# Routing and experts of a graph layer in one block instead of two, with one sequence of 98 seat transfers

## Chip, cores and metric

One core of one Trainium2 chip runs the whole program as one launch. The metric is the device time in microseconds (us). Engine names are those of the profile: PE is TensorE, DVE is VectorE, ACT is ScalarE, POOL is GpSimd, SP is SyncE, which here only issues DMAs. A "q" behind a name (SPq, POOLq) means the queue of that engine.

## What is computed

```python
xn = layernorm(x)                                  # x: 6250 x 256, fp32
x = x + gnn(xn, edges) + mix(xn)                   # two graph convolutions of three passes each; linear attention
f = layernorm(x)
rh = relu(f @ router_w1 + router_b1)               # 256 -> 128
p = softmax(rh @ router_w2 + router_b2)            # 6 experts
top_w, top_i = top_k(p, 2); w = softmax(top_w)
e_out = (relu(relu(f @ w1[e] + b1[e]) @ w2[e] + b2[e])) @ w3[e] + b3[e]   # 256 -> 256 -> 256 -> 256
x = x + sum over the two chosen experts e of w[e] * e_out[e]
```

The change touches only the last part, from the decoder of the graph network to the end (the mixture of six experts, of which each of the 6250 tokens uses two).

## The kernel before, in words

Some 2,890 us of the program are the graph part (function `sums`). The change leaves it alone, save that the 128 x 12,544-word tile `split`, which the passes used, gets a second use afterwards.

**Routing** is the function `final`, one block (L2211) in which the five engines each have an instruction list and meet through semaphores. The 49 token tiles of 128 rows go through it in 7 batches (`BATCHES`) of 7 tiles (`SUB`). For each batch PE decodes and projects, DVE adds and takes the row statistics, ACT normalises, PE turns the tiles and computes the six router logits (L2320), DVE picks the two experts (class `Choice`), and PE counts, with small products against triangular and full matrices, how many earlier tokens took the same expert (`ranked`, L2327 to L2332). From these counts DVE computes for each token two seats, that is, two row numbers in a DRAM table `row_d` that is sorted by expert, and writes them as integers (L2526, semaphore `l_idx`). POOL then sends each tile's rows (256 values, the scale and shift of the normalisation, two weights, the first expert, the token's number) to their seats: two indirect transfers per tile (L2263, `scattered`), 14 per batch. In the block of before POOL does this for the first six batches alone, 84 transfers.

After the last batch DVE does the **planning** (L2570 to L2596): from the number of tokens of each expert it makes, for each of 38 slots of 384 rows, the first row and the expert (`table`), the expert again as a number per partition (`expert_of`) and an offset that throws rows past an expert's end out of range (`beyond`). Then the block ends: every engine drains, reports to a common semaphore, and goes on when all have.

**Experts** is the function `experts`, a second block (L2650). Its POOL list begins with the 14 transfers that were left, those of the last batch (`late`, L2743). Its SP list issues the weights of slots 0 and 1 (`pack_in`, L2668, 898 KB each), waits until all 98 transfers have landed (`l_sent`), and issues the rows of slots 0 to 2 (`rows_in`, L2663). Each of these needs a row number or expert number that SP loads from `table` (L2654). For each slot DVE normalises the rows (L2692, L2694), PE turns them (L2801), ACT copies them back, PE does three layers (L2810, L2818, L2826) with ACT's relu between, DVE adds the last bias and weighs (L2716, L2720), and POOL adds the three tiles into `out` with indirect transfers (L2751). Three slots are in flight (`BUF` = 3). SP, DVE, ACT and PE run most of the 38 slots in loops of three slots; POOL's list is written out. At the end SP waits for the last of POOL's transfers, and the block ends as the first did.

Of the kernel before, what the change touches and what calls it, by code (L numbers as in the profile page):

```python
# [7 lines left out]
ALU = mybir.AluOpType  # L8
# [9 lines left out]
P = 128  # L18
# [154 lines left out]
def gps_layer(nc, a, out):  # L173
# [19 lines left out]
    with ExitStack() as whole:  # L193
# [17 lines left out]
        final(nc, a, out, sem, ident, mix, words(other)[:, NP:2 * NP], words(other), ahead, xnT_d, params, row_d, pack_d)  # L211
# [1915 lines left out]
def final(nc, a, out, sem, ident, mix, hidden, spare, ahead, xnT_d, params, row_d, pack_d):  # L2127
# [11 lines left out]
    with ExitStack() as main:  # L2139
# [5 lines left out]
        l_sent = sem("g_scattered")  # L2145
        LATE = range((BATCHES - 1) * SUB, TILES)

        with ExitStack() as ph:
# [44 lines left out]
            d_ps = [bank(f"d_ps{h}", [P, WIN]) for h in range(HB)]  # L2193
            rec_ps = [bank(f"rec_ps{n}", [P, D]) for n in range(2)]
            tn_ps = [bank(f"tn_ps{n}", [P, D]) for n in range(2)]
            lg_ps = bank("lg_ps", [P, SUB * EXP])
            rank_ps = bank("rank_ps", [P, MANY + 1, EXP])
# [13 lines left out]
            with nc.Block() as block:  # L2211
                @block.sync
                def _(sp):
# [29 lines left out]
                    sp.wait_ge(l_kept, 16 * (BATCHES + 1))  # L2243

                @block.gpsimd
                def _(pool):
# [18 lines left out]
                    for n in range(BATCHES - 1):  # L2265
                        scattered(n)

                @block.tensor
                def _(pe):
# [81 lines left out]
                    ranked(BATCHES - 1)  # L2351

                @block.scalar
                def _(act):
# [63 lines left out]
                    ratio(BATCHES - 1)  # L2418

# [178 lines left out]

        experts(nc, out, sem, ident, spare, table, beyond, expert_of, rows, seat_of, LATE, l_sent, row_d, pack_d)


def experts(nc, out, sem, ident, spare, table, beyond, expert_of, tokens, seat_of, late, l_sent, row_d, pack_d):
# [7 lines left out]
    with ExitStack() as ph:  # L2610
        def sb(name, shape, dt=F32):
            return ph.enter_context(nc.sbuf_tensor(name, shape, dt))

        def bank(name, shape):
            return ph.enter_context(nc.psum_tensor(name, shape, F32))

        rows = sb("slot_rows", [P, BUF, ST, RW])
        meta = sb("slot_meta", [P, BUF, ST, 4])
        share = sb("slot_share", [P, BUF, 3, ST])
        done = sb("slot_out", [P, BUF, ST, D])  # L2620
        space = Carve(spare)
        pack = space.take(BUF, PACK)
        idx = sb("slot_idx", [P, BUF, ST], mybir.dt.uint32)
        xlT = space.take(BUF, 2, SLOT)
        h1 = space.take(2, SLOT)
        h2 = space.take(2, SLOT)
        t_ps = [bank(f"t_ps{n}", [P, 2, 2, P]) for n in range(2)]
        one_ps = [bank(f"one_ps{n}", [P, SLOT]) for n in range(2)]
        two_ps = [bank(f"two_ps{n}", [P, SLOT]) for n in range(2)]
        out_ps = [bank(f"out_ps{n}", [P, D]) for n in range(2)]  # L2630
        k_rows, k_pack, k_sent = ([sem(f"{n}{b}") for b in range(BUF)] for n in ("k_rows_in", "k_weights_in", "k_scattered"))
        k_xl, k_turn, k_turnc, k_one, k_onec, k_two, k_twoc, k_out, k_bias, k_done, k_meta, k_share, k_idx = (
            sem(n) for n in ("k_normed", "k_turned", "k_turned_copied", "k_first", "k_first_copied", "k_second", "k_second_copied", "k_third",
                             "k_third_biased", "k_out_ready", "k_meta", "k_share", "k_idx"))

        def weight(b, n):
            return pack[:, b, n * 2 * D:(n + 1) * 2 * D].rearrange("p (c h) -> p c h", c=2)

        def bias_of(b, n, hc):
            at = 6 * D + 2 * n + hc  # L2640
            return pack[:, b, at:at + 1]

        def bias3(b):
            return pack[:, b, 6 * D + 4:6 * D + 4 + D]

        def sent(s):

            return 16 * ST * (s // BUF + 1)

        with nc.Block() as block:  # L2650
            @block.sync
            def _(sp):
                def entry(s, col):
                    _, got = nc.values_load_multi_w_load_instructions(  # L2654
                        table[0:1, bass.ds(s, 1), col:col + 1].rearrange("o s c -> o (s c)"), engines=[mybir.EngineType.SP], min_val=0,
                        max_val=(row_d.shape[0] - SLOT, EXPERTS - 1)[col],
                        skip_runtime_bounds_check_because="rows of a region and a number of an expert")
                    return got[0]

                def rows_in(s, b):  # L2660
                    at = entry(s, 0)
                    sp.wait_ge(k_turn, s + 1)
                    sp.dma_start(rows[:, b, :, :], row_d[bass.ds(at, SLOT), :].rearrange("(t p) c -> p t c", p=P)).then_inc(k_rows[b], 16)  # L2663

                def pack_in(s, b):
                    e = entry(s, 1)
                    sp.wait_ge(k_done, s * ST + ST)
                    sp.dma_start(pack[:, b, :], pack_d[bass.ds(e, 1), :, :].rearrange("o p c -> (o p) c")).then_inc(k_pack[b], 16)  # L2668

                sp.sem_inc(k_turn, BUF)  # L2670
                sp.sem_inc(k_done, BUF * ST)
                for s in range(2):
                    pack_in(s, s)
                sp.wait_ge(l_sent, 16 * 2 * TILES)
                for s in range(BUF):
                    rows_in(s, s)
                with sp.Fori(0, LOOPED) as q:
                    for b in range(BUF):
                        rows_in(q * BUF + (b + BUF), b)
                        pack_in(q * BUF + (b + 2), (b + 2) % BUF)  # L2680
                for s in range(LOOPED * BUF, STEPS - 2):
                    if s + BUF < STEPS:
                        rows_in(s + BUF, s % BUF)
                    pack_in(s + 2, (s + 2) % BUF)
                for s in range(STEPS - BUF, STEPS):
                    sp.wait_ge(k_sent[s % BUF], sent(s))

            @block.vector
            def _(dve):
                def normed(q, b):  # L2690
                    dve.wait_ge(k_rows[b], q * 16 + 16)
                    nc.vector.tensor_copy(meta[:, b, :, :], rows[:, b, :, D + 2:D + 6]).then_inc(k_meta, 1)  # L2692
                    for t in range(ST):
                        m = nc.vector.tensor_scalar(rows[:, b, t, 0:D], rows[:, b, t, 0:D], rows[:, b, t, D:D + 1], rows[:, b, t, D + 1:D + 2], ALU.mult, ALU.add)  # L2694
                    m.then_inc(k_xl, 1)

                def prepared(q, b):

                    s = q * BUF + b
                    if not (isinstance(q, int) and q == 0):  # L2700
                        dve.wait_ge(k_sent[b], q * (16 * ST))
                    dve.wait_ge(k_meta, s + 1)
                    e = expert_of[:, bass.ds(s, 1)]
                    first, second, both = (share[:, b, n, :] for n in range(3))
                    nc.vector.scalar_tensor_tensor(first, meta[:, b, :, FIRST], e, meta[:, b, :, W1], ALU.is_equal, ALU.mult).then_inc(k_share, 1)
                    nc.vector.scalar_tensor_tensor(second, meta[:, b, :, FIRST], e, meta[:, b, :, W2], ALU.not_equal, ALU.mult).then_inc(k_share, 1)
                    nc.vector.tensor_tensor(idx[:, b, :], meta[:, b, :, ID], beyond[:, bass.ds(s, 1), :].rearrange("p o t -> p (o t)"), ALU.add).then_inc(k_idx, 1)
                    dve.wait_ge(k_share, s * 3 + 2)
                    nc.vector.tensor_tensor(both, first, second, ALU.add).then_inc(k_share, 1)
                    dve.wait_ge(k_idx, s + 1)  # L2710

                def finished(q, b):
                    s = q * BUF + b
                    for t in range(ST):
                        dve.wait_ge(k_out, s * ST + (ST + t + 1))
                        nc.vector.tensor_tensor(done[:, b, t, :], out_ps[t % 2][:, :], bias3(b), ALU.add).then_inc(k_bias, 1)  # L2716
                    dve.wait_ge(k_share, s * 3 + 3)
                    for t in range(ST):
                        dve.wait_ge(k_bias, s * ST + (ST + t + 1))
                        nc.vector.tensor_scalar(done[:, b, t, :], done[:, b, t, :], share[:, b, 2, t:t + 1], None, ALU.mult).then_inc(k_done, 1)  # L2720

                for b in range(BUF):
                    normed(0, b)
# [9 lines left out]
                for s in range(LOOPED * BUF, STEPS):  # L2733
                    prepared(s // BUF, s % BUF)
                    if s + BUF < STEPS:
                        normed((s + BUF) // BUF, s % BUF)
# [137 lines left out]
```

## Time and profile before

| what | us |
|---|---|
| median of 3 runs (3478.55 to 3478.9) | 3478.65 |
| the profiled execution | 3479.78 |
| its span, first to last instruction | 3477.8 |
| PE busy in it | 3163.9 (91%) |
| POOL busy in it | 923.7 (27%) |

The profiled execution took 1.98 us more than its span, and 1.13 us more than the median. Times below are positions in the span. The columns of a row of the timeline are: start, duration, engine, line, operation, output <- inputs, shapes, count, and in brackets the idle time of the engine before it and what ended it. Several instructions of a kind that follow each other are merged into one row with their count.

### The profile page before, as it was taken

The page shows a single profiled execution, that of the slowest core. Times are in us where ns is not written, and L with a number is a line of the kernel's source. Part 1 is how long each engine was busy: PE and PEld are TensorE (multiplying, and loading weights), DVE is VectorE, ACT ScalarE, POOL GpSimd, SP SyncE. Part 2 cuts the span into 40 slices and gives each one's busy share as a digit, 9 for nine tenths or more (in the row PEclk, how much of TensorE's full clock was granted, in tenths as well). Part 3 has the DMA queues.
Part 4 walks back from the last instruction along what each step waited for, and adds up shares of the span by engine and source line. Part 5 has one row for each costly group of instructions (what it writes and reads, how often), then busy time and mean ns, then how long its engine had stood idle before and what let it go on. Part 6 is the DMA issues. An engine that isn't in the chain of part 4 may idle for free. (4 is left out here: it accounts for less than half of the span.)

```text
span 3477.8 us, 48392 instructions
## 1 busy us (share of the span) xinstructions
PE 3163.9 (91%) x16879; PEld 1851.0 (53%) x16880; DVE 1374.4 (40%) x5337; ACT 787.6 (23%) x1656; POOL 923.7 (27%) x912
## 2 busy tenths in 40 slices
PE   7798999999998898898999999999999999728998
PEld 3464666566554444454455555555555556516775
DVE  7846777777732222221222221222221005433443
ACT  3444555555520000000000000000000003313332
POOL 2000000000006666636666630000000000454555
PEclk9897999999998999999999999999999999869999
DMA  7212465556457666756666668888889995336886
GB/s 185 72 65 85 149 235 208 179 198 234 179 234 246 196 222 203 235 179 203 211 211 223 212 188 291 291 290 292 291 292 319 303 302 160 118 111 168 204 203 138
DMA packets 252700, 723.78 MB, mean 208 GB/s; under 512 B 36437, under 2 KB 159817, under 8 KB 250472
## 3 DMA queue, kind: packets, MB, share of 16 engines
q1 hardware_dynamic: 184298, 595.84, 51.1%
q0 software_dynamic: 53216, 112.76, 11.7%
q10 hardware_dynamic: 15006, 12.82, 1.3%
q8 instruction: 109, 1.79, 0.2%
q14 instruction: 71, 0.58, 0.0%
HBM read 543.01 MB, written 189.34 MB: 211 GB/s over the span
## 5 line engine op out<-in xcount | busy, mean ns | idle before, releaser
L1886 PE MATMUL first_sum<-stage,split 128*128 128x448 f16 (+1 forms) x4508 | 933.3, 355 | 31.4 <-issue 29.1
L1886 PEld LDWEIGHTS first_sum<-stage,split 128*128 128x128 f16 x4508 | 443.6, 99 | 448.4 <-issue 63.7
L1886 PE MATMUL first_sum<-stage,other 128*128 128x448 f16 (+1 forms) x3136 | 664.8, 354 | 15.7 <-issue 15.5
L1836 PE MATMUL first_sum<-stage,other 128*128 128x448 f16 x2744 | 649.9, 354 | 0.2 <-ACT stage L1360 0.2
L1345 POOL DMA_INDIRECT stage<-fresh_d,lane_two x324 | 308.4, 952 | 1117.2 <-DMA fresh_d<-split 942.0
L1886 PEld LDWEIGHTS first_sum<-stage,other 128*128 128x128 f16 x3136 | 309.6, 99 | 298.3 <-issue 35.4
L1360 ACT ACTIVATE stage<-group_ps 128x392 f16<-128x392 f32 x784 | 385.4, 497 | 297.9 <-PE group_ps L1825 294.7
L1345 POOL DMA_INDIRECT stage<-later_d,lane_two x324 | 307.7, 950 | 220.4 <-issue 71.5
L1513 DVE TENSOR_SCALAR place<-iota_col,rel 128x196 f16<-128x196 f16 x1568 | 348.8, 265 | 0.0
L1836 PEld LDWEIGHTS first_sum<-stage,other 128*128 128x128 f16 x2744 | 254.0, 98 | 139.5 <-issue 2.0
L1932 PE MATMUL group_ps<-stage,place 128*128 128x512 f16 x720 | 265.8, 385 | 11.3 <-issue 7.3
L1510 DVE TENSOR_TENSOR lanes<-iota_two,lane_two 128x256 f16<-128x256 f16 x784 | 225.0, 287 | 83.3 <-PE group_ps L1825 71.5
L1821 PE MATMUL group_ps<-place,lanes 128*128 128x196 f16 x784 | 199.9, 255 | 33.4 <-DVE place L1513 14.7
L2247 POOL IOTA ids<- 128x49 f32 x1 | 0.2, 173 | 841.2 <-POOLq L1233 841.2
L2751 POOL DMA_INDIRECT out<-slot_out,slot_idx x114 | 176.5, 1548 | 163.9 <-DMA out<-slot_out,slot_idx 92.7
L1632 DVE TENSOR_SCALAR place<-iota_col,lane_two 128x128 f16<-128x128 f16 x720 | 145.8, 272 | 156.8 <-PE group_ps L1932 111.9
L1825 PE MATMUL group_ps<-place,lanes 128*128 128x196 f16 x784 | 200.9, 257 | 0.0
L2360 ACT ACTIVATE dT<-d_ps,rel 128x448 f32<-128x448 f32 x14 | 8.8, 633 | 843.2 <-PE d_ps L2278 814.1
L1710 DVE TENSOR_TENSOR stage<-first_sum,stage 128x448 f32<-128x448 f32 x42 | 26.2, 625 | 390.7 <-PE first_sum L1886 377.0
L1821 PEld LDWEIGHTS group_ps<-place,lanes 128*128 128x128 f16 x784 | 77.7, 99 | 113.5 <-ACT stage L1360 43.5
L2716 DVE TENSOR_TENSOR slot_out<-out_ps,other 128x256 f32<-128x256 f32 x114 | 48.4, 425 | 185.7 <-PE out_ps L2826 180.0
L2263 POOL DMA_INDIRECT row_d<-rows,seat_idx x84 | 83.8, 998 | 126.0 <-DVE seat_idx L2526 101.9
(387 smaller groups left out, 3052.6 us busy)
## 6 DMA issues: line engine op xcount, KB each, us to landing
stage<-adj_d SPq DMA_DIRECT2D x420, 784.0 KB
adj_d<-stage SPq DMA_DIRECT2D x14, 5488.0 KB, 18.5
row_d<-slow_rows SPq DMA_DIRECT2D x12, 3340.5 KB
other<-pack_d SPq DMA_DIRECT2D x38, 898.0 KB
slot_rows<-row_d SPq DMA_DIRECT2D x38, 393.0 KB
stage<-root_d SPq DMA_DIRECT2D x18, 448.0 KB
xnT_d<-other SPq DMA_DIRECT2D x14, 448.0 KB
split<-root_d SPq DMA_DIRECT2D x14, 448.0 KB, 3.8
```

The lines of the kernel that those rows point to most:

```text
L1345: nc.gpsimd.indirect_dma_start(got[:, g % GOT, :, :].rearrange("p s c -> p (s c)"), None, tables_d[t].rearrange("p j s c -> (p j) (s c)"), ...
L1360: nc.scalar.activation(stage[w % 2][:, :, at * G:(at + 1) * G], group_ps[g % BANKS][:, 0:COLS].rearrange("p (d h) -> p h d", d=G), ACT.Cop ...
L1510: nc.vector.tensor_tensor(lanes[:, u % 4, :, :], iota_two[:, :, :], lane_two[:, bass.ds(g, 1), :].broadcast_to([P, P, 2]), ALU.is_equal)
L1513: nc.vector.tensor_scalar(place[:, 2 * u % RING + s, :], iota_col[:, 0:Q4], rel[:, :, :, :].rearrange("p q s g -> p (q s g)")[:, bass.ds(p ...
L1632: nc.vector.tensor_scalar(hot[:, h % HOTS, :], iota_col[:, s % 2 * P:s % 2 * P + P], tab_key[:, at:at + 1], None, ALU.is_equal).then_inc(s ...
L1821: mm(group_ps[u % BANKS][:, 0:Q4], lanes[:, u % 4, :, 0], place[:, 2 * u % RING, :], start=True, stop=True, skip_group_check=True)
L1825: return mm(group_ps[u % BANKS][:, Q4:COLS], lanes[:, u % 4, :, 1], place[:, 2 * u % RING + 1, :], start=True, stop=True, skip_group_check ...
L1836: m = mm(acc[b][k][:, 0:WIN], other[:, h, half, k * P:(k + 1) * P], stage[b][:, h, :], start=(h == 0 and half == 0), stop=(h == TILES - 1 ...
L1886: m = mm(acc[b][k][:, lo:WIN], side(t)[:, h, part, k * P:(k + 1) * P], ring[:, i, r, lo:WIN], start=(h == 0 and part == 0), stop=(h == TIL ...
L1932: m = mm(group_ps[S % 2][:, :], hot[:, h % HOTS, :], got[:, g % GOT, :, :].rearrange("p s c -> p (s c)"), start=(n == SPANS[s % 2][0]), st ...
L2263: nc.gpsimd.indirect_dma_start(row_d[:, :], bass.IndirectOffsetOnAxis(ap=seat_of[:, j, which:which + 1], axis=0), rows[:, j, :], None).the ...
L2751: nc.gpsimd.indirect_dma_start(out[:, :], bass.IndirectOffsetOnAxis(ap=idx[:, b, t:t + 1], axis=0), done[:, b, t, :], None, bounds_check=N ...
```

## The change

- `experts` becomes `slot_engines`, which allocates nothing and opens no block; it returns five functions, one for each engine, and the routing block calls each at the end of that engine's list.
- POOL's loop over `scattered` runs over all 7 batches, so that the 98 seat transfers are one sequence. The list `late` and its 14 transfers in the second block go.
- Between the planning and the slots there is no drain and no meeting of the engines. DVE raises a new semaphore, `l_table`, at the end of the planning, and SP waits for it before `slots.sync`.
- The slot buffers (`slot_rows`, `slot_meta`, `slot_share`, `slot_out`, `slot_idx`) are carved from `split` instead of being allocated.
- Eight whole PSUM banks are allocated once; routing and slots use views of them.

```diff
-        l_sent = sem("g_scattered")
-        LATE = range((BATCHES - 1) * SUB, TILES)
+        l_sent, l_table = sem("g_scattered"), sem("g_slots_known")
...
-            d_ps = [bank(f"d_ps{h}", [P, WIN]) for h in range(HB)]
-            rec_ps = [bank(f"rec_ps{n}", [P, D]) for n in range(2)]
...
+            banks = [bank(f"bank{n}", [P, 512]) for n in range(8)]
+            d_ps = [banks[h][:, 0:WIN] for h in range(HB)]
+            rec_ps = [banks[2 + n][:, 0:D] for n in range(2)]
...
+            slots = slot_engines(nc, out, sem, ident, spare, slot_space, table, beyond, expert_of, banks, row_d, pack_d)
...
                     sp.wait_ge(l_kept, 16 * (BATCHES + 1))
+                    sp.wait_ge(l_table, 1)
+                    slots.sync(sp, l_sent)
...
-                    for n in range(BATCHES - 1):
+                    for n in range(BATCHES):
                         scattered(n)
+                    slots.gpsimd(pool)
...
                     ranked(BATCHES - 1)
+                    slots.tensor(pe)
...
                     ratio(BATCHES - 1)
+                    slots.scalar(act)
...
                     v.settle()
-
-        experts(nc, out, sem, ident, spare, table, beyond, expert_of, rows, seat_of, LATE, l_sent, row_d, pack_d)
+                    dve.sem_inc(l_table, 1)
+                    slots.vector(dve)
...
-        rows = sb("slot_rows", [P, BUF, ST, RW])
-        done = sb("slot_out", [P, BUF, ST, D])
+    rows = spot.take(BUF, ST, RW)
+    done = spot.take(BUF, ST, D)
...
-        t_ps = [bank(f"t_ps{n}", [P, 2, 2, P]) for n in range(2)]
+    t_ps = [banks[n][:, :].rearrange("p (t k n) -> p t k n", t=2, k=2) for n in range(2)]
...
-                for j in late:
-                    for which in range(2):
-                        nc.gpsimd.indirect_dma_start(row_d[:, :], bass.IndirectOffsetOnAxis(ap=seat_of[:, j, which:which + 1], axis=0), tokens[:, j, :], None).then_inc(l_sent, 16)
```

The bodies of the five slot lists are the same instruction for instruction.

## Rows read from the trace of the kernel before

**Rows 1.** Busy time by stage: routing, the seam, the slots.

```profile
core 0: us, PE busy (x) PEld busy (x) DVE busy (x) ACT busy (x) POOL busy (x), PEclk, DMA share, GB/s
2893.00:3117.00 224.00, 145.51 (x679) 106.56 (x677) 105.38 (x418) 76.25 (x158) 84.80 (x91) 0.79 0.39 129
3117.00:3140.00 23.00, 0.00 (x0) 0.00 (x0) 0.33 (x2) 0.00 (x0) 13.44 (x14) 0.50 0.56 194
3140.00:3477.00 337.00, 322.51 (x1292) 226.27 (x1292) 137.33 (x531) 121.34 (x228) 176.46 (x114) 0.98 0.72 180
```

**Rows 2.** Timeline around the seam, all engines.

```profile
3103.00 0.96 POOL L2263 DMA_INDIRECT row_d<-rows,seat_idx  x1 [0.30 <-issue]
...
3108.64 0.20 DVE L2522 TENSOR_TENSOR seats<-rank_ps,taken 128x42 f32<-128x42 f32 x1 [6.93 <-remote]
...
3109.51 0.17 DVE L2526 CAST seat_idx<-seat 128x14 uint32<-128x14 f32 x1
...
3115.65 0.20 DVE L2596 TENSOR_SCALAR beyond<-past 128x114 f32<-128x114 f32 x1
3117.04 0.96 POOL L2743 DMA_INDIRECT row_d<-rows,seat_idx  x1 [13.08 <-POOLq L2211]
3117.18 1.24 SPq L2668 DMA_DIRECT2D other<-pack_d  x2
...
3133.48 0.96 POOL L2743 DMA_INDIRECT row_d<-rows,seat_idx  x1 [0.30 <-issue]
3136.39 6.56 SPq L2663 DMA_DIRECT2D slot_rows<-row_d  x4
3139.67 0.17 DVE L2692 COPY slot_meta<-slot_rows 128x12 f32<-128x12 f32 x1 [23.82 <-DMA slot_rows<-row_d]
...
3140.86 1.54 PE L2801 MATMUL t_ps<-ident,slot_rows 128*128 128x128 f32 x6 [42.90 <-DVE slot_rows L2694]
```

**Rows 3.** Timeline of an earlier batch: its seats and its first transfer.

```profile
3068.41 0.17 DVE L2526 CAST seat_idx<-seat 128x14 uint32<-128x14 f32 x1
...
3068.86 0.96 POOL L2263 DMA_INDIRECT row_d<-rows,seat_idx  x1 [4.97 <-DVE seat_idx L2526]
```

**Rows 4.** Instructions of the block's own line L2211: nanoseconds, first and last start.

```profile
L2211 POOLq DRAIN x1: 22078/22078/22078, 3088.8 to 3088.8; - x1
L2211 DVEq DRAIN x1: 24/24/24, 3116.1 to 3116.1; - x1
```

**Rows 5.** Timeline: a POOL transfer beside a long DVE addition, in batch 1.

```profile
2987.24 0.96 POOL L2263 DMA_INDIRECT row_d<-rows,seat_idx  x1 [12.72 <-DVE seat_idx L2526]
...
2994.01 2.02 DVE L2429 TENSOR_TENSOR rows<-rows,rel 128x1792 f32<-128x1792 f32 x1
2994.85 2.01 POOL L2263 DMA_INDIRECT row_d<-rows,seat_idx  x1 [0.30 <-issue]
...
3004.75 0.96 POOL L2263 DMA_INDIRECT row_d<-rows,seat_idx  x1 [0.30 <-issue]
```

**Rows 6.** Timeline: POOL in batch 5, first transfer, and beside two DVE steps.

```profile
3086.56 0.96 POOL L2263 DMA_INDIRECT row_d<-rows,seat_idx  x1 [0.30 <-issue]
...
3096.15 0.19 DVE L2512 COPY rows<-m 128x7 f32<-128x7 f32 x1
...
3096.39 0.17 DVE L2516 TENSOR_SCALAR m<-m 128x7 f32<-128x7 f32 x1
3096.68 0.96 POOL L2263 DMA_INDIRECT row_d<-rows,seat_idx  x1 [0.31 <-issue]
```

**Rows 7.** Busy time by stretch of the seam.

```profile
3117.00:3126.00 9.00, 0.00 (x0) 0.00 (x0) 0.00 (x0) 0.00 (x0) 6.83 (x8) 0.50 0.83 292
3126.00:3137.00 11.00, 0.00 (x0) 0.00 (x0) 0.00 (x0) 0.00 (x0) 6.61 (x7) 0.50 0.28 100
```

**Rows 8.** Timeline of PE in the first slots.

```profile
3144.76 3.54 PE L2810 MATMUL one_ps<-other 128*128 128x384 f32 x8
...
3151.01 0.82 PE L2801 MATMUL t_ps<-ident,slot_rows 128*128 128x128 f32 x6
...
3159.42 0.82 PE L2801 MATMUL t_ps<-ident,slot_rows 128*128 128x128 f32 x6
```

**Rows 9.** Waits of the routing stage that no instruction in the profile explains.

```profile
DVE lg L2467 <- remote: 36.8, 4, 16.0
DVE seats L2522 <- remote: 8.7, 2, 6.9
DVE rows L2517 <- remote: 3.6, 1, 3.6
```

More of the change, by code:

```diff
@@ L1 @@
+from collections import namedtuple
 from contextlib import ExitStack
@@ L210, in gps_layer @@
              (fresh_d, later_d), row_d, pack_d)
[L211 removed]
+        final(nc, a, out, sem, ident, mix, words(other)[:, NP:2 * NP], words(other), words(split), ahead, xnT_d, params, row_d, pack_d)
 def sums(nc, a, sem, ident, dinv, mix, split, other, rel, params, ahead, adj_d, lin_d, runs_d, bounds_d, deg_d, dinv_d, xnT_d, root1_d, starts_d,
@@ L2124, in newton, with final @@
     v.then(nc.vector.scalar_tensor_tensor(to, to, 1.5, root, ALU.add, ALU.mult))
-def final(nc, a, out, sem, ident, mix, hidden, spare, ahead, xnT_d, params, row_d, pack_d):
+def final(nc, a, out, sem, ident, mix, hidden, spare, slot_space, ahead, xnT_d, params, row_d, pack_d):
     EXP = EXPERTS
@@ L2597, in _, with slot_engines @@
                     v.settle()
-        experts(nc, out, sem, ident, spare, table, beyond, expert_of, rows, seat_of, LATE, l_sent, row_d, pack_d)
-def experts(nc, out, sem, ident, spare, table, beyond, expert_of, tokens, seat_of, late, l_sent, row_d, pack_d):
+                    dve.sem_inc(l_table, 1)
+                    slots.vector(dve)
+SlotEngines = namedtuple("SlotEngines", "sync gpsimd tensor scalar vector")
+def slot_engines(nc, out, sem, ident, spare, slot_space, table, beyond, expert_of, banks, row_d, pack_d):
     RW = ROWW
@@ new lines, in slot_engines @@
+    spot = Carve(slot_space)
+    rows = spot.take(BUF, ST, RW)
+    meta = spot.take(BUF, ST, 4)
+    share = spot.take(BUF, 3, ST)
+    done = spot.take(BUF, ST, D)
+    idx = spot.take(BUF, ST, dt=mybir.dt.uint32)
+    space = Carve(spare)
+    pack = space.take(BUF, PACK)
+    xlT = space.take(BUF, 2, SLOT)
+    h1 = space.take(2, SLOT)
+    h2 = space.take(2, SLOT)
+    t_ps = [banks[n][:, :].rearrange("p (t k n) -> p t k n", t=2, k=2) for n in range(2)]
+    one_ps = [banks[2 + n][:, 0:SLOT] for n in range(2)]
@@ new lines, in slot_engines @@
+    two_ps = [banks[4 + n][:, 0:SLOT] for n in range(2)]
+    out_ps = [banks[6 + n][:, 0:D] for n in range(2)]
+    k_rows, k_pack, k_sent = ([sem(f"{n}{b}") for b in range(BUF)] for n in ("k_rows_in", "k_weights_in", "k_scattered"))
+    k_xl, k_turn, k_turnc, k_one, k_onec, k_two, k_twoc, k_out, k_bias, k_done, k_meta, k_share, k_idx = (
+        sem(n) for n in ("k_normed", "k_turned", "k_turned_copied", "k_first", "k_first_copied", "k_second", "k_second_copied", "k_third",
+                         "k_third_biased", "k_out_ready", "k_meta", "k_share", "k_idx"))
@@ new lines, in gpsimd @@
+    def gpsimd(pool):
+        for s in range(STEPS):
+            b = s % BUF
+            pool.wait_ge(k_idx, s + 1)
+            if s >= 1:
+                pool.wait_ge(k_sent[(s - 1) % BUF], sent(s - 1))
+            for t in range(ST):
+                pool.wait_ge(k_done, s * ST + (BUF * ST + t + 1))
+                nc.gpsimd.indirect_dma_start(out[:, :], bass.IndirectOffsetOnAxis(ap=idx[:, b, t:t + 1], axis=0), done[:, b, t, :], None,
+                                             bounds_check=N - 1, oob_is_err=False, compute_op=ALU.add).then_inc(k_sent[b], 16)
@@ new lines, in scalar, with turned, first, second @@
+    def scalar(act):
+        def turned(s, b):
+            act.wait_ge(k_turn, s + (BUF + 1))
+            nc.scalar.activation(xlT[:, b, :, 0:2 * P].rearrange("p k (t n) -> p t k n", t=2), t_ps[0][:, :, :, :], ACT.Copy)
+            nc.scalar.activation(xlT[:, b, :, 2 * P:3 * P], t_ps[1][:, 0, :, :], ACT.Copy).then_inc(k_turnc, 1)
+        def first(s, b):
+            for hc in range(2):
+                act.wait_ge(k_one, s * 2 + (hc + 1))
+                act.wait_ge(k_two, s * 2 + 2)
+                nc.scalar.activation(h1[:, hc, :], one_ps[hc][:, :], ACT.Relu, bias=bias_of(b, 0, hc)).then_inc(k_onec, 1)
+        def second(s, b):
+            for hc in range(2):
+                act.wait_ge(k_two, s * 2 + (hc + 3))
+                act.wait_ge(k_out, s * ST + ST)
+                nc.scalar.activation(h2[:, hc, :], two_ps[hc][:, :], ACT.Relu, bias=bias_of(b, 1, hc)).then_inc(k_twoc, 1)
+        act.sem_inc(k_two, 2)
+        act.sem_inc(k_out, ST)
+        turned(0, 0)
+        turned(1, 1)
+        first(0, 0)
+        with act.Fori(0, (STEPS - 2) // BUF) as q:
+            for b in range(BUF):
+                s = q * BUF + b
+                second(s, b)
+                turned(s + 2, (b + 2) % BUF)
+                first(s + 1, (b + 1) % BUF)
+        for s in range((STEPS - 2) // BUF * BUF, STEPS):
+            b = s % BUF
+            second(s, b)
+            if s + 2 < STEPS:
+                turned(s + 2, (b + 2) % BUF)
+            if s + 1 < STEPS:
+                first(s + 1, (b + 1) % BUF)
@@ L2851 @@
+    return SlotEngines(sync, gpsimd, tensor, scalar, vector)
 _INS = ["x", "src", "dst"] + [f"L0_gnn_{n}" for n in (
```

349 lines of the change are left out of this document (140 added, 209 removed).

## Prediction

> **What bounds the kernel now.** I read the last 585 us by stage first [rows 1]. Routing takes 224 us in which no engine is full. The slots take 337 us, of which PE is busy for 322.5: they are bound by PE, one slot every 3159.42 - 3151.01 = 8.41 us [rows 8]. Between the two lie 23 us in which PE and ACT do nothing, DVE does two instructions and POOL issues its 14 late transfers. The timeline then shows the seam itself as one chain without slack [rows 2]. DVE gets the last counts at 3108.64, writes the last seats by 3109.68 (3109.51 + 0.17), and ends the planning at 3115.85. The block ends and POOL starts the 14 transfers at 3117.04. The last one starts at 3133.48 and ends at 3134.44. 1.95 us later, at 3136.39, SP issues the first rows, which reach DVE at 3139.67, and PE starts at 3140.86. What a reader should see is the bracket of L2743: POOL stood still for 13.08 us, up to the block's own line L2211, although all it needs, the seats, was there 7.36 us before its start. The planning sits in the chain only because the block's end makes POOL wait for DVE.
>
> **The change part by part.**
>
> *Transfers of the last batch start with their seats.* In the one sequence POOL waits for `l_idx` alone; the wait for `l_row` was met before the seats were. In an earlier batch the seats were written by 3068.58 and the first transfer began at 3068.86, after POOL had stood for 4.97 us [rows 3]: 0.28 us. So the 14 transfers start at 3109.68 + 0.28 = 3109.96 instead of 3117.04. Gain: 7.08 us. One row could delay this: POOL's drain at the block's end, issued at 3088.8, ended at 3088.8 + 22.08 = 3110.88 [rows 4], 6.9 us behind its last transfer. The drain itself goes with the block; but if it shows POOL at work on its earlier transfers until then, the start is 3110.88 and the gain 6.16. I take 7.08, since the start in rows 3 came just as promptly 4.97 us after a batch, when by that reading POOL was not done; 6.16 stays as the near end.
>
> *The 14 transfers now run beside the planning.* Their pace alone is (3133.48 - 3117.04)/13 = 1.265 us [rows 2]. Beside DVE it can be worse: in batch 1 one transfer took 2.01 us instead of 0.96 while DVE did an addition of two SBUF operands that lasts 2.02 us, and the batch took 3004.75 - 2987.24 = 17.51 instead of 16.44 from first start to last [rows 5]. The planning has no such long step. Its longest are three products and comparisons of two SBUF operands at about 0.39 us each, and all of it lasts 6.14 us. Nearest in size are the steps of the choice, 0.2 to 0.24 us each, and beside some twenty of them batch 5 took 3103.00 - 3086.56 = 16.44 us, no more than alone [rows 2, 6]. Ends: nothing, and 3 x 0.39 = 1.2 us if each long step holds a transfer for its full length. The planning's steps are nearer to those of the choice than to the 2.02 us one, so I take 0.1 us.
>
> The Trainium skill (SBUF — State Buffer, "Who interferes with whom") says that DVE's copies, casts and tensor-scalar steps can lock GpSimd out of a shared SBUF port and so starve the descriptors of indirect DMAs, and it infers that tensor-tensor steps do not. The trace disagrees in one half: the step that held POOL in rows 5 is a tensor-tensor, and the gap behind the copy and the tensor-scalar in rows 6 is 0.31 instead of 0.30 us. By the page the price would be the planning's small copies and tensor-scalars; by the rows it is near nothing, and I keep it as a rival.
>
> *Weights earlier, but later against the transfers.* SP's first weights went out at 3117.18, 1.33 us after the planning's end at 3115.85; through a semaphore instead of the meeting they go at about 3116.9. They took until 3126 (292 GB/s until then, 100 after) [rows 7]: 8.8 us, so 3125.7 now. The last transfer ends at 3127.4 in the new order, so its landing is again free of them, and I leave the 1.95 us to SP's row issue as they are. PE needs the weights 3.9 us after its first turn (3144.76 against 3140.86) [rows 2, 8], which is 3137.8 now: 12 us of cover. Cost nothing.
>
> *The planning itself* no longer lies on the chain. Its cover: SP reads `table` for the first rows at 3136.39 - 7.0 = 3129.4, and the planning ends at 3115.9 as before, 13 us earlier. If it is held for longer than that, the gain shrinks one for one.
>
> *The meeting, the drains and the second entry* go, 3115.85 to 3117.04, about 1.2 us. This is part of the 7.08 and is not counted twice. SP's new wait on `l_table` has only the weights and rows behind it, both priced.
>
> *Memory and banks.* Other addresses for the slot buffers and the same eight banks in the same order; the slot bodies are unchanged and bound by PE. No row prices a change there. The bound is what a moved address could do to a DMA's landing, and rows are fetched three slots ahead. I take 0, and 0.5 us either way for the range.
>
> *PE's clock.* PE is idle for 42.9 us before the first slot and would be for 36; it is at 0.50 of full clock, 1.2 GHz, in the whole seam [rows 1], so the slots start at the same level. Cost nothing.
>
> **Sum.** 7.08 - 0.1 = 7.0 us. The slots then follow with everything 7 us earlier, POOL's last transfer too. Span 3477.8 - 7.0 = 3470.8; that execution 3479.78 - 7.0 = 3472.8. It lay 1.13 above the median of the runs, so against that 3478.65 - 7.0 = 3471.6 us.
>
> About 0.2% (6.96 us) is what a measurement of this kernel can tell from no change. The forecast stands on that line, which the chances must show.
>
> **The rivals.**
>
> *A. POOL is held by the planning's small steps.* The rule above as a mechanism: eight copies, casts and tensor-scalars from L2573 to L2596, of which the last is 0.20 us [rows 2] and the nearest kin 0.17 and 0.19 [rows 6], each hold a transfer for their whole length, 8 x 0.17 = 1.4 us. Gain 5.6, time 3473.0. Against it stands the pace of batch 5; for it, that rows 5 show that DVE can hold POOL at all. Chance 0.10.
>
> *B. Slower: the planning is held until the transfers have passed.* Beside the seat transfers of routing DVE waited 16.0, 6.9 and 3.6 us at steps where no instruction in the profile explains it [rows 9]; the 6.9 ended at 3108.64, 4.7 us behind the end of POOL's last transfer (3103.96) [rows 2]. Before, the planning ran in the quiet between two rounds of transfers. If it is held in the same way it starts 4.7 us behind 3127.4, at 3132.1, ends 6.1 us later at 3138.2, and SP issues weights at 3139.2. Rows queued behind both weights, at 8.8 us, arrive at 3148.0 instead of 3139.67: 8.3 us slower, 3487.0. It decides only from 13 us of holding on. Against it: of the planning's kind, steps that depend on DVE's own last step, only L2517 was ever held beside transfers, once for 3.6 us. Chance 0.04, and milder forms that eat one or two us are in the forecast's lower half.
>
> *C. It does not start earlier.* If the last batch's transfers wait for something else that came only with the meeting, nothing moves: 3478.7. All that POOL touches was there; chance 0.03.
>
> *D. More than the seam.* The waits of rows 9 before the seam are 6.9 and 3.6 us in the last batch; if they depend on what stands next in each engine's list (a drain now, the slots then), they may go: up to 10.5 us more, 3461.1. Everything ahead of the seam is the same, instruction by instruction, so 0.05.
>
> **How the numbers follow.** The forecast has 0.78: gains of 6.1 to 7.6, of which a little more than half lie above 6.96 (0.43) and the rest below (0.35). Faster by over 0.2%: 0.43 and D's 0.05, 0.48. Within 0.2%: 0.35, A's 0.10 and C's 0.03, 0.48. Slower: B, 0.04. The range goes from 3469.8 (1.1 us for what moved code and addresses do besides the 0.5) to 3474.2 (A with the long steps' 1.2 us on top). It leaves out B, C, D and a few hundredths of the forecast.
>
> **What the profile after should show.** POOL one row of 98 at one line, the 85th starting within 0.3 us of the seats at 3109.7, at a pace of 1.265; the planning's last step still at 3115.7; SP's rows out at about 3129.4; PE's first turn at 3133.8 with about 36 us idle before it; 8.41 us per slot; the end at 3470.8. The prediction is wrong if the 85th transfer starts near 3111 (the drain's reading), if single transfers take over 0.96 while the planning runs (A), if the planning's end moves beyond 3125 (B), or if the slots start 7 us earlier and the end does not.

## The result and the profile after

| | before | changed |
|---|---|---|
| median of 18 runs each, us | 3476.67 | 3468.97 |
| range of the runs | 3467.38 to 3483.99 | 3461.43 to 3476.1 |
| profiled execution | 3479.78 | 3473.0 |
| its span | 3477.8 | 3471.1 |

The ratio is 0.9978, with a 95% interval of 0.9968 to 0.9988: 7.7 us faster, between 4.2 and 11.1. In a second set (e13 below) it was 0.9984 (0.9975 to 0.9994), 5.6 us. Both intervals hold the 7.0 us of the forecast. The predicted time did not hold: 3468.97 lies under the range's low end of 3469.8. The kernel before measured 3476.67 over 18 runs, 2 us under the three runs that the forecast started from.

Busy time by stage in the changed kernel, the same three stages as in [rows 1]:

```profile
core 0: us, PE busy (x) PEld busy (x) DVE busy (x) ACT busy (x) POOL busy (x), PEclk, DMA share, GB/s
2895.00:3111.00 216.00, 139.81 (x679) 102.68 (x679) 101.38 (x395) 76.32 (x158) 85.43 (x93) 0.82 0.40 133
3111.00:3134.00 23.00, 0.00 (x0) 0.00 (x0) 5.85 (x28) 0.00 (x0) 13.42 (x14) 0.50 0.56 192
3134.00:3471.00 337.00, 322.55 (x1292) 226.26 (x1292) 137.32 (x531) 121.47 (x228) 176.46 (x114) 0.98 0.73 180
```

The 23 us in which POOL sends its last 14 transfers are still there, but nearly all of DVE's planning (5.85 us) now lies inside them; in rows 1 it lay ahead of them. The slots are the same 322.5 us of PE.

The timeline around the seam, answering to [rows 2]:

```profile
3109.56 0.20 DVE L2529 TENSOR_TENSOR seats<-bank,taken 128x42 f32<-128x42 f32 x1 [10.40 <-remote]
...
3110.42 0.17 DVE L2533 CAST seat_idx<-seat 128x14 uint32<-128x14 f32 x1
...
3110.87 0.96 POOL L2267 DMA_INDIRECT row_d<-rows,seat_idx  x1 [5.80 <-DVE seat_idx L2533]
...
3114.67 1.04 POOL L2267 DMA_INDIRECT row_d<-rows,seat_idx  x1 [0.30 <-issue]
...
3115.34 0.36 DVE L2594 TENSOR_SCALAR s_of<-s_of 128x38 f32<-128x38 f32 x1
...
3116.82 0.23 DVE L2603 TENSOR_SCALAR beyond<-past 128x114 f32<-128x114 f32 x1
...
3118.18 1.34 SPq L2670 DMA_DIRECT2D other<-pack_d  x2
...
3127.42 0.96 POOL L2267 DMA_INDIRECT row_d<-rows,seat_idx  x1 [0.30 <-issue]
3130.38 6.54 SPq L2665 DMA_DIRECT2D split<-row_d  x4
3133.64 0.17 DVE L2693 COPY split<-split 128x12 f32<-128x12 f32 x1 [16.60 <-DMA split<-row_d]
...
3134.83 1.54 PE L2796 MATMUL bank<-ident,split 128*128 128x128 f32 x6 [39.86 <-DVE split L2695]
```

Measured from the last seats (the end of the cast), the 85th transfer starts after 0.28 us instead of 7.36, and PE's first turn comes after 24.24 us instead of 31.18: the seam gives 6.94 us. The whole difference of the two profiled executions is three terms: -6.94 in the seam, +0.91 because the seats themselves came later in this execution (3110.59 against 3109.68), and -0.66 behind PE's last turn, in POOL's last transfers (PE's first to last turn is 305.0 us in both). Together -6.7, as the spans say. The absolute places that were forecast for this profile (rows out at 3129.4, PE's first turn at 3133.8 after 36 us of idle time) came about a us later, at 3130.38 and 3134.83, mostly because the seats did; PE's idle time was 39.9 us, for the most part because the last batch's counts took longer to reach DVE (10.40 us at L2529 against 6.93).

### The profile page after: what moved, and what is told of

Same layout as the page of the kernel before. It is cut to its first block and busy times, and to the rows that moved or that the text cites. A ratio compares the mean times of both kernels' runs of the same rounds, so it can differ in the third digit from the quotient of the medians.

```text
span 3471.1 us, 48381 instructions
## 1 busy us (share of the span) xinstructions
PE 3156.9 (91%) x16879; PEld 1844.1 (53%) x16880; DVE 1371.1 (39%) x5337; ACT 787.7 (23%) x1656; POOL 926.0 (27%) x912
## 5 line engine op out<-in xcount | busy, mean ns | idle before, releaser
L1933 PE MATMUL group_ps<-stage,place 128*128 128x512 f16 x720 | 265.9, 386 | 11.2 <-issue 6.8
L2748 POOL DMA_INDIRECT out<-split x114 | 176.5, 1548 | 163.3 <-DMA out<-split 89.0
L2366 ACT ACTIVATE dT<-bank,rel 128x448 f32<-128x448 f32 x14 | 8.8, 634 | 843.6 <-PE bank L2283 813.7
L2267 POOL DMA_INDIRECT row_d<-rows,seat_idx x98 | 97.6, 996 | 133.2 <-DVE seat_idx L2533 105.1
L2717 DVE TENSOR_TENSOR split<-bank,other 128x256 f32<-128x256 f32 x114 | 48.6, 426 | 186.1 <-PE bank L2821 179.5
```

The source lines that it names most:

```text
L1933: m = mm(group_ps[S % 2][:, :], hot[:, h % HOTS, :], got[:, g % GOT, :, :].rearrange("p s c -> p (s c)"), start=(n == SPANS[s % 2][0]), st ...
L2267: nc.gpsimd.indirect_dma_start(row_d[:, :], bass.IndirectOffsetOnAxis(ap=seat_of[:, j, which:which + 1], axis=0), rows[:, j, :], None).the ...
L2748: nc.gpsimd.indirect_dma_start(out[:, :], bass.IndirectOffsetOnAxis(ap=idx[:, b, t:t + 1], axis=0), done[:, b, t, :], None, bounds_check=N ...
```

## The experiments

Each is a small edit of the kernel named. Seam times are counted from the end of the last cast of the seats, since the seats themselves move from execution to execution.

**e1: the early start taken away, the single block kept.** Base: the changed kernel.

```diff
                     for n in range(BATCHES):
+                        if n == BATCHES - 1:
+                            pool.wait_ge(l_table, 1)
                         scattered(n)
```

> One block as in the changed kernel, but POOL waits for the end of the planning (l_table) before the 14 transfers of the last batch. Theory (the gain is the early start of these 14): their first one starts about 0.3 us after the planning's end, some 6.5 us after the seats; first PE turn about 30.4 us after the seats, against 24.2 in the changed kernel and 31.2 in the one before; time about 1 us under the kernel before, 6 above the changed one. Rival (the gain is the block's end itself, its drains and its meeting): the time stays with the changed kernel, 7 under the one before.

Measured: ratio to the kernel before 0.9987 (0.9973 to 1.0001), 4.5 us with an interval that reaches 0; the 1 us expected lies inside it. The timeline, with the last seats at 3092.90:

```profile
3099.41 0.96 POOL L2267 DMA_INDIRECT row_d<-rows,seat_idx  x1 [11.90 <-DVEq L2607]
...
3123.26 1.54 PE L2798 MATMUL bank<-ident,split 128*128 128x128 f32 x6 [47.22 <-DVE split L2697]
```

The transfers start 6.51 us after the seats and PE turns after 30.36 us, as the theory said to 0.1 us. Of the 6.94 us of the seam, 6.1 come from the early start and 0.8 from the meeting itself. The rival falls by these rows; the timed ratio alone could not have settled it.

**e2: one sequence of 98, but two blocks.** Base: the kernel before.

```diff
-        LATE = range((BATCHES - 1) * SUB, TILES)
+        LATE = range(0)
...
-                    for n in range(BATCHES - 1):
+                    for n in range(BATCHES):
                         scattered(n)
```

> Two blocks as before, but all 98 seat transfers stand in the first. Theory (the block's end makes SP and the weights wait for POOL): the 14 transfers start 0.3 us after the seats, but the meeting comes only after POOL's drain, which ends between 0 and 7 us after the last transfer (17.4 us after the first); weights and rows are issued together behind it, so that rows queue with 1.8 MB of weights. First rows at DVE between 24 and 33 us after the seats, against 30.0 in the kernel before and 23.1 in the changed one; time between 5 us under and 4 us above the kernel before. Rival (one sequence of 98 is all there is to it, one block is not needed): 7 us under the kernel before.

Measured: ratio 1.0009 (0.9994 to 1.0024). The timeline, with the last seats at 3091.88:

```profile
3092.16 0.96 POOL L2263 DMA_INDIRECT row_d<-rows,seat_idx  x1 [5.66 <-DVE seat_idx L2526]
...
3108.69 0.96 POOL L2263 DMA_INDIRECT row_d<-rows,seat_idx  x1 [0.30 <-issue]
3118.77 1.24 SPq L2668 DMA_DIRECT2D other<-pack_d  x2
3120.51 2.09 SPq L2663 DMA_DIRECT2D slot_rows<-row_d  x3
3126.86 0.17 DVE L2692 COPY slot_meta<-slot_rows 128x12 f32<-128x12 f32 x1 [28.53 <-DMA slot_rows<-row_d]
```

The block's own line L2211 in the same kernel (nanoseconds, start):

```profile
L2211 POOLq DRAIN  x1: 23305/23305/23305, 3094.4 to 3094.4; - x1
```

POOL starts as early as in the changed kernel, and nothing is won: the drain ends at 3117.7, 8.1 us behind the end of the last transfer, the weights go out only then, and the rows behind them need 6.35 us to reach DVE instead of 3.3. PE turns 36.16 us after the seats, 5.0 later than before. DVE's 34.97 us are 2 over what was expected. The ratio has no clear sign, so the cost is read from the seam alone. One sequence without one block costs there; the two parts of the change need each other.

**e4: a longer planning.** Base: the changed kernel. The added steps multiply by 1.0.

```diff
                     v.settle()
+                    for _ in range(36):
+                        v.then(ts(past[:, :, :], past[:, :, :], 1.0, None, ALU.mult))
                     dve.sem_inc(l_table, 1)
```

> The changed kernel with 36 more dependent steps of 0.20 us at the planning's end (the values are not changed), about 8.5 us. Theory (13 us of cover): weights out 8.5 us later, at about 17 us after the seats, rows out and first PE turn as in the changed kernel, 24.2 us after the seats, within 1.5 us; the weights now lie beside the last transfers and may delay their landing by about a us. Rival (the planning is on the chain): the first PE turn comes 8.5 us later.

One execution. The added steps, by shortest, median and longest in nanoseconds:

```profile
L2606 DVE TENSOR_SCALAR past<-past x36: 220/222/442, 3093.2 to 3104.1; 128x114 f32<-128x114 f32 x36
```

The timeline behind them, with the last seats at 3086.70:

```profile
3106.68 1.24 SPq L2672 DMA_DIRECT2D other<-pack_d  x2
3108.41 2.41 SPq L2667 DMA_DIRECT2D split<-row_d  x3
3115.32 0.17 DVE L2695 COPY split<-split 128x12 f32<-128x12 f32 x1 [10.81 <-DMA split<-row_d]
```

Both expectations miss. The steps took 11.3 us instead of 8.5: nine of the 36 lasted 0.43 to 0.44 us, one for each transfer beside them (1.9 us together), and even undisturbed ones began every 0.26 us, where 8.5 allows 0.24. The planning ended 11.4 us later than in the changed kernel, still inside the 13 us of cover that I had given it, and PE turned 29.81 us after the seats, 5.6 us late. The rows went out 21.7 instead of 19.8 us after the seats, and reached DVE 6.9 us after their issue instead of 3.3, beside the weights: from 3106.7 to 3115 the DMA engines were 88% busy at 302 GB/s. The cover of the planning is a good deal under 11 us: SP issues both weights ahead of the rows, and rows that go out before the weights are through arrive late. In the changed kernel the weights went out at 3118.18 and, with the 8.8 us of rows 7, were through at about 3127.0, 3.4 us before the rows. By this estimate the cover without any cost is 3.4 us.

**e8: the memory alone.** Base: the kernel before, `slot_rows`, `slot_meta`, `slot_share`, `slot_out` and `slot_idx` carved from `split`.

```diff
-        rows = sb("slot_rows", [P, BUF, ST, RW])
+        spot = Carve(slot_space)
+        rows = spot.take(BUF, ST, RW)
```

> The kernel before, in two blocks, with the slot buffers in the passes' tile as in the changed kernel. Theory (memory costs and gives nothing): first PE turn 31.2 us after the last seats, slots 305.0 us from first to last turn, no difference from the kernel before that 5 rounds can tell. Rival (the place of the buffers gives a part of the gain): over 0.7 us in the slots or their landings.

Measured: ratio 1.0013 (1.0000 to 1.0027). PE's first turn 31.21 us after the seats, 305.06 us from first to last turn: the seam and the slots are those of the kernel before within 0.1 us. The ratio leans to slower by 4.5 us with an interval that touches 1, and nothing in the two stages that use the memory answers to it; I read it as spread between executions, and no run settles that.

**e3: routing without transfers.** Base: the changed kernel.

```diff
+                    pool.wait_ge(l_idx, BATCHES)
                     for n in range(BATCHES):
```

> The changed kernel, with POOL held until the seats of the last batch are written, so that routing runs without a seat transfer beside it. Theory R (the unexplained waits of DVE and ACT in routing come from the seat transfers beside them): the waits of over 1.5 us marked remote go, the last seats are written up to 25 us earlier, near 3085; then all 98 transfers take 124 us, and the end comes some 80 us later. Rival S (they come from PE's own small matmuls at half clock): the waits stay, last seats at 3109 to 3111, end some 106 us later.

One execution, 3500.76 us, against a kernel before of 3457.09. First the unexplained waits of routing in the changed kernel (total us, times, longest), as in [rows 9]:

```profile
DVE lg L2474 <- remote: 32.6, 4, 13.2
...
ACT dT L2366 <- remote: 19.8, 2, 10.9
DVE seats L2529 <- remote: 12.1, 2, 10.4
ACT rhT L2392 <- remote: 4.5, 2, 2.3
```

In e3 no wait of this stage is marked remote. The instructions on the seats there (nanoseconds, first and last start):

```profile
L2267 POOL DMA_INDIRECT row_d<-rows,seat_idx x98: 956/960/1111, 3030.8 to 3153.8; - x98
L2534 DVE CAST seat_idx<-seat x7: 174/175/175, 2936.6 to 3030.3; 128x14 uint32<-128x14 f32 x7
```

From the first seats to the last it takes 93.8 us. In the changed kernel it takes 152.8 (2957.6 to 3110.4). Theory R stands, and the size was underrated: the seats come 59 us earlier, where up to 25 were expected, and so the last transfer starts 47 us later than in the changed kernel, counted from the first seats, and not 80. Busy times between the first and the last seats, of the changed kernel, of e3 and of e6 (below):

```profile
2957.60:3110.40 152.80, 83.38 (x413) 58.99 (x411) 60.39 (x259) 48.71 (x102) 84.02 (x84) 0.75 0.33 110
2936.60:3030.30 93.70, 76.90 (x413) 55.28 (x411) 58.58 (x259) 48.45 (x102) 0.00 (x0) 0.88 0.19 59
2942.60:3037.00 94.40, 75.67 (x413) 54.26 (x412) 59.07 (x260) 48.46 (x102) 51.10 (x53) 0.89 0.40 133
```

PE's granted clock is lower beside the transfers (0.75 of full clock on the mean of the stretch, against 0.88), but PE is busy for only 6.5 us more and DVE for 1.8, so most of the 59 us are waits. Most of them follow steps of PE. The traces also record when a semaphore changes: in the changed kernel the update that ends the wait at L2529 comes 14.6 us behind the modelled end of PE's last product, and in e3 no such update is over 0.02 us behind. One of DVE's own updates was 3.6 us late in the kernel before (the wait at L2517); no update of ACT's that ended a wait was over 0.02 us late in any run. PE's ends are modelled, so it stays open whether PE's work or only its semaphore was late.

**e6, e7, e9, e10: how many transfers may be under way.** Base: the changed kernel. POOL's transfers take `n` semaphores in turn, and POOL issues one only when the n-th before it has landed.

```diff
+                                if k >= n:
+                                    pool.wait_ge(l_sent[k % n], 16 * (k // n))
-                                nc.gpsimd.indirect_dma_start(...).then_inc(l_sent, 16)
+                                nc.gpsimd.indirect_dma_start(...).then_inc(l_sent[k % n], 16)
```

> The same with one transfer at a time: each waits for the landing of the one before. Pace about 0.3 + 0.96 + 1.4 = 2.7 us, 98 transfers 265 us from the first, so 120 us longer than the changed kernel if nothing else moves. Theory Q: PE's updates within 1 us, last seats near 94 us after the first. Theory T: delays stay over 5 us.

> The changed kernel, but POOL issues a seat transfer only when the one before the last has landed (two semaphores in turn), so that no more than two stand in its queue or in flight. With all transfers held, the updates of PE's semaphores came within 0.02 us of the modelled end; beside bursts of 14 they came up to 14.6 us late. Theory Q (the burst, a queue of transfers that runs ahead, delays the other engines' semaphores): the delays fall under 2 us, the last seats come 20 to 55 us earlier after the first ones (153 us in the changed kernel, 94 with all held), POOL's pace stays within 0.4 us of 1.27, and the time falls by 15 to 45 us. Theory T (each transfer delays them, queued or not): the delays stay over 5 us; the slower pace costs up to 30 us.

> The changed kernel with at most three seat transfers queued or in flight (three semaphores in turn). With two in flight routing ran almost undelayed (last seats 94 us after the first) and POOL became the bound, at 1.40 to 2.22 us for each transfer, because it often waited for a landing. Theory Q: with three the landings are covered, the pace falls to 1.27 to 1.5 us, the delays of PE's updates stay mostly under 2 us, and the last transfer starts 125 to 145 us after the first (163 with two, 169 in the changed kernel): 25 to 45 us under the changed kernel. Rival (three are a burst already): delays of 5 to 15 us come back, and the time lies within 8 us of the changed kernel.

> The same with at most four. Theory Q: pace 1.27 to 1.35 us; delays larger than with three, since the queue is what makes them: between those of three in flight and of the changed kernel. Rival (only a queue of many transfers delays): as good as or better than three.

| at most under way | first to last seats, us | first to last transfer, us | ratio to before (95%) |
|---|---|---|---|
| no limit (changed kernel) | 152.8 | 169.3 | 0.9978 (0.9968 to 0.9988) |
| 1 (e7) | 94.4 | 293.7 | one execution, 3584.98 us against 3454.84 |
| 2 (e6) | 94.4 | 163.2 | 0.9985 (0.9975 to 0.9994) |
| 3 (e9) | 141.2 | 161.2 | 0.9953 (0.9940 to 0.9967) |
| 4 (e10) | 138.8 | 157.7 | 0.9958 (0.9942 to 0.9973) |

e6 and e7 were measured on one chip, e9 and e10 on another, the changed kernel in a set of its own, so only the ratios can be compared. With one or two under way routing runs almost as if there were no transfers (the latest of PE's updates is 0.4 us late in e7 and 1.3 in e6), and POOL is the bound: two waited too often for a landing, with 163.2/97 = 1.68 us each, and one took 3.0 us each where 2.7 was expected. e6 moves more data per us between its first and last seats than the changed kernel (133 against 110 GB/s) and starts as many transfers per us (53 in 94.4 us, 84 in 152.8), so it is not their mean rate that holds the other engines. Its gain is about 5 us; the 15 to 45 us expected did not come. Three and four are about 15 us under the kernel before, but e9 misses the 25 to 45 us under the changed kernel: by the ratios it is 9, close to what its rival said (three are a burst already). In both the last batch was held again, by PE updates up to 19.1 us late in e9 and 20.2 in e10. e10's delays are not clearly larger than e9's, and neither is its time, against theory Q. The waits of e10:

```profile
POOL row_d L2270 <- DVE seat_idx L2536: 85.8, 5, 60.5
...
DVE lg L2477 <- remote: 31.2, 1, 31.2
ACT rhT L2395 <- remote: 26.8, 3, 16.1
DVE seats L2532 <- remote: 9.8, 1, 9.8
```

One wait of 31.2 us for the logits of the last batch. It lies where batches 4 and 5 were sent without any pause, at 1.26 us each, because their landings were always in time. A limit of three or four that is never reached there does nothing. It does not show that the number under way is without effect: in e7 a transfer took 2.5 us (median) from its start to its landing, so that in a stream at 1.26 us each about two are under way when the next starts, three in all. By this estimate e9 and e10 had three under way in these batches, and e6 never more than two.

**e11, e12, e13: pauses where the last batch needs them.** As e10, but the number under way is set per batch: four for batches 0 to 3, no limit for the last; two in batches 4 and 5 (e11) or in batch 4 alone (e12). e13 is the changed kernel again, on the same chip.

```diff
+                        abreast = [4, 4, 4, 4, 2, 4, 0][n]
...
+                                if abreast and k >= abreast:
+                                    pool.wait_ge(l_sent[(k - abreast) % 4], 16 * ((k - abreast) // 4 + 1))
```

> The changed kernel with at most four seat transfers queued or in flight in batches 0 to 3, two in batches 4 and 5, no limit in the last. With three or four throughout, batches 4 and 5 ran without a pause at 1.26 us and the last batch's logits came 14 to 19 us late, so that POOL stood for 11.6 us before the last 14. Theory Q' (it is a stretch of transfers without a pause that delays the updates, not the number in flight): with two in flight batches 4 and 5 take 1.4 us each, 40 instead of 35 us, the delay falls under 3 us, the last seats are there before batch 5 is sent and the last 14 follow without a stop: the last transfer starts about 5 to 8 us earlier than with four, about 150 us after the first, and the time is 5 to 8 us under that with four. Rival (the delay stays): 2 to 8 us above it.

> The same with two in flight in batch 4 alone and four in batch 5. Theory Q': the pauses lie where the last batch's logits are made, so the delay is under 3 us here too, and the last transfer starts 2 us earlier than with two in both. Rival: a delay of over 8 us is back and POOL stands before the last 14.

> The changed kernel itself, on the same chip as the two above. Theory (the seam is a fixed 7 us in every run, whatever the level of the chip): the ratio to the kernel before lies between 0.9970 and 0.9990, about 7 us; first PE turn 24.2 us after the last seats, the 14 transfers 0.28 us after them, slots 305.0 us from first to last turn. Rival (the 7.7 us measured first were partly chance in the waits of routing): the ratio differs from 0.9978 by more than 0.001 while the seam stays.

| | median, us | ratio to before (95%) | last seats to 85th transfer, us |
|---|---|---|---|
| before, this chip | 3476.26 | | |
| e13, changed kernel | 3471.30 | 0.9984 (0.9975 to 0.9994) | 0.28 |
| e11 | 3457.78 | 0.9948 (0.9930 to 0.9966) | 18.89 |
| e12 | 3454.77 | 0.9941 (0.9924 to 0.9957) | 23.43 |

The waits of e12:

```profile
ACT dT L2370 <- remote: 8.1, 1, 8.1
DVE rows L2456 <- remote: 7.3, 2, 4.3
DVE seats L2533 <- remote: 6.0, 2, 4.1
ACT rhT L2396 <- remote: 3.2, 2, 2.3
```

The long wait for the logits is gone: PE's update for them is 1.2 us late in e12 and 1.8 in e11, against 14.3 in e10, though DVE still waited 7.6 us for them in e11. In e12 the last seats are ready 23 us before POOL gets to them, and the last transfer starts 156.7 us after the first, against 169.6 in e13. Theory Q' holds in its main point for both: a limit of two where the last batch's logits are made removes that delay. Whether the pauses do it or the lower number under way is not separated, since a limit of two gives both; no run has pauses with three under way, or two under way without a pause. The 5 to 8 us under e10 are not shown, since no run has e10 on this chip: the first to last transfer is 1.0 us shorter than in e10 for e12, 2.8 longer for e11, and the intervals of the ratios overlap. e12 (four executions) beats the kernel before by 21.5 us and the changed one by 16.5, by medians on one chip; against four throughout it is no clear gain.

e13 shows the seam again at its fixed size: 0.28 us to the 85th transfer, 24.24 us to PE's first turn. Its ratio lies in the expected 0.9970 to 0.9990.

## Why the prediction was right, and where it was wrong

- **The start of the last 14 transfers** (7.08 us) was right: 0.28 us after the seats, as in rows 3, in the changed kernel, in e2, e4 and e13. The drain's reading (POOL at work until 6.9 us behind its last transfer, gain 6.16) falls: in the changed kernel POOL stood for only 5.80 us and still began 0.28 us after the seats.
- **The price beside the planning** (0.1 us) was right in size: 13 intervals took 16.55 us instead of 16.44. Its sign did show once, as one transfer of 1.04 instead of 0.96 us (1.05 in e2, e4 and e13), which is most of the 0.11 us; rival A's 1.4 us are out. The planning itself became 0.27 us longer beside the transfers: L2594 took 0.36 us instead of 0.18, and in e4 steps of 0.22 us took up to 0.44. The Trainium skill (SBUF — State Buffer, "Who interferes with whom") says that DVE's two-port modes, which a tensor-scalar step can enter, contend with GpSimd, and that whoever issues first keeps the shared ports for the whole instruction while the other is fully blocked. The doubled tensor-scalar steps agree in kind; their length does not show it, for a step gained at most 0.22 us beside a transfer of 0.96.
- **Weights, clock, banks, memory**: nothing, as said. The last landing and SP's row issue took 2.00 us instead of 1.95; e8 has the memory alone at 0 in seam and slots (31.21 against 31.18 us, 305.06 against 304.96).
- **The meeting** was counted inside the 7.08. e1 gives it by itself: 0.8 us, where I had written about 1.2.
- **The planning's cover** was mis-sized. I gave it 13 us and said that rival B decides only from there on. In e4 an end 11.4 us later cost 5.6 us. What failed in it is the reading of "SP reads `table` for the first rows" as the only deadline: the weights stand ahead of the rows in SP's list and share the DMA engines with them. In the changed kernel this cost nothing, since the planning ended 6.4 us after the seats, about 3.4 us before it would have begun to.
- **The time** was outside the range, and the step that failed is the last one of the sum, "against that 3478.65": the level that the gain is taken from. The gain of 7.0 us was taken from a level of three runs that lay within 0.35 us of each other, with 0.5 and 1.1 us allowed for everything else, and nothing for the level itself. (From 3471.6 these two give a low end of 3470.0; the 3469.8 on record is 0.2 below its own terms.) Over 18 runs the same kernel spans 16.6 us, and its median was 3476.67, 3457.09, 3454.84, 3454.44 and 3476.26 us in the five sets of this study. The profiled executions show where some of it lies. The spans of the kernel before and of e8, whose seam and slots are equal, differ by 20.2 us: 15.0 of it lie ahead of the first seats (2955.6 against 2940.6), in stages that no variant touches, and 4.8 between the first seats and the last. Rows 9 held the warning, and I used them only for a rival: waits of 16, 7 and 4 us that no instruction explains are waits that can be different in the next execution. They also showed DVE's alone; ACT's waits of this kind were 38.4 us more. With 3476.67 for 3478.65 the sum gives 3469.7, 0.7 from what was measured. The size of the gain was right; that so little is left over is luck, since the ratio leaves the gain open between 4.2 and 11.1 us. What moves the level of the earlier stages stays open.
- **The chances** of 0.48 and 0.48 on both sides of 0.2% fit: 0.22% in one set, 0.16% in the other. Rival D did not happen: the waits of the last batch stayed (10.4 us at L2529 against 6.9). Rival B did not happen, C neither.

## What to carry to other kernels

Where a block ends, look at which engine had its inputs long before: the gain of merging was almost wholly one producer's wait (6.1 of 6.9 us), and moving the work across without removing the meeting lost it again (e2). Measure a seam from its own first event, not from the span: two executions of one kernel here differed by more than the change is worth. When engines wait with no cause in the profile, hold back whatever runs beside them in one variant: that showed 59 us, eight times the change.

## What the runs showed of the hardware

- Beside a stream of POOL's indirect transfers at 1.26 us each, PE releases the next engine late: up to 14.6 us behind its modelled end in the changed kernel and 20.2 in e10, with single waits of up to 33.2 us (e9). PE's drain at the block's end, row below, began with the last small products and lasted 11.2 us, to the moment at which DVE went on (3108.64). With all transfers held (e3), one under way (e7) or two (e6) no wait marked remote was left. Three and four under way left fewer of them, but no less in total (76.3 and 73.4 us over all engines, 69.0 in the changed kernel); a limit of two in one or two batches left 24.6 (e12) and 49.0 (e11).
- What in the stream delays them is open. No run separates POOL's issuing from the data it moves, or pauses from the number under way. A part of the profiler in it is not excluded either: every time here comes from a profiled execution, and the trace of e7 holds all 1568 semaphore updates of the 98 landings, that of the changed kernel 379, so records are lost where the transfers are dense.
- POOL's drain ends well behind its last indirect transfer: 6.9 us before (3110.88 against 3103.96), 8.1 in e2.
- A DVE addition of two SBUF operands (2.02 us) lengthened the transfer beside it by 1.05 us [rows 5], and in two more batches by 0.99 and 1.06. A DVE tensor-scalar of 0.22 us took 0.44 once per transfer (e4).

The drain of PE in the kernel before, nanoseconds and start:

```profile
L2211 PEldq DRAIN  x1: 11218/11218/11218, 3097.4 to 3097.4; - x1
```
